# Feed-forward in groups of four, three and one token tiles in place of four, two and two

## The reference

```python
h = jnp.square(jax.nn.relu(jnp.einsum('bsd,fd->bsf', x, W_fc)))
y = jnp.einsum('bsf,df->bsd', h, W_proj)
# five steps of a neuron, from mem = 0:
#   mem = 0.9 * mem + y - (mem > 1);  spike = (mem > 1)
# result of the feed-forward: the sum of the five spikes / 5
```

## Time and profile before

| | |
|---|---|
| median of 3 runs | 1944.62 us (1941.21 to 1946.56) |
| profiled execution | 1942.4 us |
| its span | 1940.6 us |
| mean granted clock of PE | 0.984 |
| PE matmul busy | 1865.1 us, 96% |
| DVE busy | 1160.5 us, 60% |
| ACT busy | 834.9 us, 43% |
| POOL busy | 858.2 us, 44% |

### The profile page before, as it was taken

The page is one execution under the profiler, slowest core; times in us unless marked ns, Lnnn a source line. Parts: engine busy times, 40 slices in busy tenths (PEclk is TensorE's granted clock), DMA queues, the critical chain, the costliest instruction groups (busy, mean ns, idle before and its releaser), DMA issues. The chain is left out here.

```text
span 1940.6 us, 65596 instructions
## 1 busy us (share of the span) xinstructions
PE 1865.1 (96%) x28992; PEld 1605.5 (83%) x28992; DVE 1160.5 (60%) x1418; ACT 834.9 (43%) x1032; POOL 858.2 (44%) x830
## 2 busy tenths in 40 slices
PE   6999999999999999999999999999999989689998
PEld 3889898989888888888888989898989768567887
DVE  4375766657574848484848474757575561754265
ACT  4444444445453535353545354545444322324322
POOL 0192636454454536372727272727273520544111
PEclk9999999999999999999999999999999999879999
DMA  5200202011020202020202020202020130222110
GB/s 208 84 4 3 75 3 75 14 64 43 35 72 6 76 2 76 3 76 3 75 3 75 3 75 3 75 3 75 3 74 3 67 120 22 56 71 87 55 55 23
DMA packets 38829, 94.55 MB, mean 49 GB/s; under 512 B 18592, under 2 KB 18592, under 8 KB 38304
## 3 DMA queue, kind: packets, MB, share of 16 engines
q1 hardware_dynamic: 38560, 90.26, 13.5%
HBM read 81.99 MB, written 6.16 MB: 45 GB/s over the span
## 5 line engine op out<-in xcount | busy, mean ns | idle before, releaser
L378 POOL TENSOR_TENSOR fold<-fold,prob 128x256 f32<-128x256 f32 (+1 forms) x704 | 686.6, 975 | 55.2
L98 PE MATMUL ring<-y_parts,wk_s 128*128 128x402 f32 (+1 forms) x3072 | 609.1, 351 | 3.7 <-PEq L151 3.7
L98 PE MATMUL ring<-wv_s,y_parts 128*128 128x512 f32 (+1 forms) x2496 | 598.1, 397 | 0.0
L98 PEld LDWEIGHTS ring<-y_parts,wk_s 128*128 128x128 f32 x3072 | 553.0, 189 | 19.8 <-issue 6.0
L98 PEld LDWEIGHTS ring<-wv_s,y_parts 128*128 128x128 f32 (+1 forms) x2496 | 455.1, 184 | 113.2
L372 POOL TENSOR_TENSOR fold<-prob 128x256 f32<-128x256 f32 x64 | 66.4, 1037 | 729.9 <-ACT prob L415 729.9
L392 ACT ACTIVATE k_sb<-ring 128x402 f32<-128x402 f32 (+1 forms) x256 | 129.4, 506 | 376.5 <-PE ring L98 376.5
L528 DVE TENSOR_TENSOR prob<-prob,diag 128x1024 f32<-128x1024 f32 (+1 forms) x192 | 276.9, 1495 | 13.5 <-ACT diag L411 13.5
L405 ACT ACTIVATE prob<-s_ps 128x1536 f32<-128x1536 f32 (+1 forms) x128 | 199.9, 1562 | 137.9 <-PE s_ps L645 137.8
L415 ACT ACTIVATE prob<-prob 128x1024 f32<-128x1024 f32 (+1 forms) x192 | 206.7, 1123 | 0.9 <-DVE prob L528 0.9
L645 PEld LDWEIGHTS s_ps<-q_sb,k_sb 32*64 32x64 f32 x13312 | 155.9, 130 | 35.8 <-issue 35.8
(11 more groups left out here) (143 smaller groups left out, 1540.4 us busy)
## 6 DMA issues: line engine op xcount, KB each, us to landing
y_raw<-yT SPq DMA_DIRECT2D x48, 804.0 KB, 7.3
y_raw<-yT SPq DMA_DIRECT2D x16, 792.0 KB, 9.9
f_raw<-w_ffn SPq DMA_DIRECT2D x22, 512.0 KB, 3.2
p_x<-x SPq DMA_DIRECT2D x2, 1024.0 KB, 7.0
q_scratch<-p_x SPq DMA_DIRECT2D x4, 512.0 KB, 2.6
q_sb<-q_scratch SPq DMA_DIRECT2D x16, 128.0 KB, 7.8
x_sb<-x SPq DMA_DIRECT2D x4, 512.0 KB, 8.2
v_sw<-y_raw SPq DMA_DIRECT2D x4, 512.0 KB, 9.6
```

What stands on the lines that cost most here:

```text
L98: mm = pe.matmul(out, left(a, c), right(b, c), start=(c == 0 and n == 0), stop=(c == DC - 1 and n == 2))
L378: pool.tensor_tensor(acc[0:m], acc[0:m], prob[0:m, i, t, :], ALU.add).then_inc(sum_step, 1)
```

## The change

`GROUPS` becomes four, three and one tile, with banks 0 to 2 for the second group and bank 3 for the last. The moving side of the first layer is then 384 columns in the second group and 128 in the third. The last group's one tile has its neuron steps done in two halves of 256 columns that alternate, in place of two tiles of 512 that alternate, and they all wait for the last matmul; the semaphore `last_first` is gone.

```diff
--- before.py
+++ after.py
@@ -1153,9 +1153,9 @@
     FB = FF // P
     STEPS, BETA = 5, 0.9
 
-    GROUPS = [range(0, 4), range(4, 6), range(6, 8)]
+    GROUPS = [range(0, 4), range(4, 7), range(7, 8)]
     LAST_TILES = GROUPS[-1]
-    BANKS = [(0, 1, 2, 3), (0, 1), (2, 3)]
+    BANKS = [(0, 1, 2, 3), (0, 1, 2), (3,)]
     ALL = len(GROUPS) * FB
     LEVELS = spike_levels(STEPS, BETA)
     OPS = STEPS + 1
@@ -1189,7 +1189,6 @@
                                                           sem("f_sq"), sem("f_h_hi"), sem("f_h_lo"))
         y_part, y_out, spike, done, stored = (sem("f_y_part"), sem("f_y_out"), sem("f_spike"), sem("f_done"),
                                               sem("f_stored"))
-        last_first = sem("f_last_first")
         block = ctx.enter_context(nc.Block())
 
         def load_of(n):
@@ -1279,12 +1278,12 @@
 
         @block.vector
         def _(dve):
-            def neuron(t, k, y, total):
+            def neuron(t, k, y, total, at=slice(0, D)):
 
                 if k == 0:
                     return dve.tensor_scalar(total, y, LEVELS[0], None, ALU.is_gt)
                 if k == STEPS:
-                    return dve.scalar_tensor_tensor(x_sb[:, t, :], total, 1.0 / STEPS, x_sb[:, t, :],
+                    return dve.scalar_tensor_tensor(x_sb[:, t, at], total, 1.0 / STEPS, x_sb[:, t, at],
                                                     ALU.mult, ALU.add)
                 return dve.scalar_tensor_tensor(total, y, LEVELS[k], total, ALU.is_gt, ALU.add)
 
@@ -1347,18 +1346,16 @@
 
 
             q = OPS * LAST_TILES[0]
+            t = LAST_TILES[0]
+            dve.wait_ge(y_part, ALL)
             for k in range(OPS):
-                for j, t in enumerate(LAST_TILES):
-                    if k == 0 and j == 0:
-                        dve.wait_ge(last_first, 1)
-                    elif k == 0:
-                        dve.wait_ge(y_part, ALL)
+                for half in range(2):
+                    at = slice(half * D // 2, (half + 1) * D // 2)
                     dve.wait_ge(spike, q - 1)
-                    neuron(t, k, y_ps[BANKS[-1][j]][:], acc[:, 1 + j, :]).then_inc(spike, 1)
+                    neuron(t, k, y_ps[BANKS[-1][0]][:, at], acc[:, 1, at], at).then_inc(spike, 1)
                     q += 1
-            for j in range(len(LAST_TILES)):
-                dve.wait_ge(spike, q - 1 + j)
-                dve.sem_inc(done, 1)
+            dve.wait_ge(spike, q)
+            dve.sem_inc(done, 1)
 
         @block.tensor
         def _(pe):
@@ -1387,8 +1384,6 @@
                         mm = pe.matmul(y_ps[bank][:], h_s[:, n % HS, a, k * P:(k + 1) * P],
                                        place_of(load_of(n))[:, b, D:2 * D],
                                        start=(f == 0 and m == 0), stop=(f == FB - 1 and m == 2))
-                    if n == ALL - 1 and k == 0:
-                        mm.then_inc(last_first, 1)
                 mm.then_inc(y_part, 1)
 
             norm.pe_products(pe, range(TT - 2))
```

## The result

The changed kernel takes 1950.66 us (median of 22 runs, 1944.91 to 1960.83), the kernel before 1943.01 us (22 runs beside it, 1938.54 to 1949.56). The ratio is 1.0045 with a 95% interval from 1.0031 to 1.0060: slower by about 8.7 us (the medians lie 7.7 us apart), against the +5.4 us of the sum. The profiled execution of the changed kernel took 1946.96 us, its span is 1945.1 us: 4.5 us more than the span before.

What follows compares the result with a forecast made beforehand. PE, busy 96% of the span, was taken as the bound. Terms 9.8 - 2.9 + 1.0 + 0.2 - 2.5 - 0.2 = +5.4 us gave 1947.8, or 1950.0 us at the median; range 1943.0 to 1971.5.

Steps and rivals of the forecast that it cites:

- First layer, group of three: First-layer matmuls of 384 columns in the second group: half way between 1.42 and 2.72, 2.07 us a block, 33.1 us.
- First layer, last group: First-layer matmuls of 128 columns: 1.38 us a block, 22.1 us; both groups' first layers together +9.8 us.
- the load is the pace: Last group's first layer: weight load sets the matmul's pace, about 0.115 us each, so halving columns buys almost nothing.
- Rival B: Last group's first layer: narrow matmuls fall to the full-precision price, 2.7 us for 12; +25.4 us, 1970.0, chance 0.30.
- rival C: Last group's first layer: narrow matmuls as quick as their columns, 0.77 us for 12; -0.5 us, 1944.1, chance 0.15.
- Second layer: Second-layer matmuls of groups two and three: 192 of the same shape before and after, 0.23 us each, cost zero.
- The old stall gone: Second group: PE's 2.9 us of waits for f_h, with DVE held beside POOL's subtractions, disappear; -2.9 us, bounds -2.9 and 0.
- Rival D: Feed-forward: the stall between POOL and DVE stays or moves, 2.9 us kept; +8.3 us, 1952.9, slower, chance 0.10.
- The new waits: Last group: DVE late beside POOL in three blocks, +1.0 us, bounds 0 and 3; low half at the very end, +0.2.
- There each low half can wait for POOL: Last group, three blocks where POOL subtracts: DVE's low half of h is delayed, 0.3 to 0.4 us lost in each.
- The end: After the last matmul: twelve 256-column neuron steps take 4.2 us, -2.5 us; one store lands instead of two, -0.2.
- case A: The forecast itself: +5.4 us, 1950.0 at the median, own range 1947.5 to 1952.5, chance 0.42.

## Why the prediction was right, and where it was off

- **First layer, group of three:** 2.07 us a block forecast, 2.10 measured.
- **First layer, last group:** 1.38 forecast from the load's pace, 1.29 measured. The step "the load is the pace" is shown by the two runs that double the columns and the loads. Its price was taken between 0.109 and 0.118; it is 0.1075. Rival B, the full-precision price (2.7 us), and rival C (0.77 us) are out. The line through 256 and 512 columns ends where the load begins.
- **Second layer:** forecast zero, measured +0.7 us: 0.74 for three matmuls, not 0.69. The term was mis-sized. Three matmuls take 0.69 to 0.70 when matmuls of 256 columns go before, 0.74 after 128 and 0.78 after 64, so it lies in the change from narrow matmuls to wide ones.
- **The old stall gone:** -2.9 forecast, -3.4 measured. The mechanism held, and the size was the idle time between records, which is less than what a wait costs from start to start. Rival D is out for the group of three.
- **The new waits:** +1.0 for the low half beside POOL and +0.2 at the end were forecast; 2.1 and 0.3 came. The step that fell short is "There each low half can wait for POOL": the last neuron step of a tile can too, since it adds to x and reads two operands from SBUF. It fell beside POOL and cost 1.2 us, as the run that holds it back shows. Nor is 0.3 to 0.4 us a limit for the low half: with three steps a block it waited for most of a subtraction, and PE 1.78 us.
- **The end:** -2.5 and -0.2 forecast, -2.6 and -0.2 measured.
- **The sum:** +5.4 forecast, +5.9 in the profiles. That they lie so near is in part luck: the first layers came 1.0 us under their term and the stall 0.5 under, the second layer 0.7 and the new waits 1.2 over. The 1950.0 us forecast at the median, beside 1950.66 measured, is luck as well: it stands on a median of the kernel before that was 1.6 us above that of the 22 runs. The rest of the measured +8.7 us (1.0045, 1.0031 to 1.0060) was in no term: I costed one execution, at full clock, and gave no chance to a fall of the clock in the last group. It is shown that such a fall is possible there (half clock from a gap of 1.78 us on, about +12 us). That the upper group of the changed kernel is this same fall was not seen in a trace and stays open: in all six profiles with the gap of 1.2 us the clock stays full, and that no run of 12 without this gap lies in the upper group can be chance.
- **The chances:** case A was given 0.27 for no difference and 0.15 for slower. The mechanism was A's, and the time came out on the slower side, just beyond the 0.3% that I had named.

## What to carry to other kernels

In this number format, with the weights standing for one matmul only, a matmul of 64 or 128 columns costs as much as its weight load (by the line through 256 and 512 columns, an estimate, anything below some 230 does); splitting tokens unevenly into groups makes the narrow group pay that in full, and here a shorter end (2.6 us) was bought with 16 x 12 matmuls that shrink by a tenth for half the columns (+8.8 us for both groups together). Before regrouping work to shorten a tail, look at what stalls in the middle: moving neuron steps away from POOL's subtractions gave 0.2 to 0.3% with no change of PE's work. And on an engine that shares a port, sort the instructions by where their operands lie, one by one, the last of a series too.

## What the runs showed of the hardware that was not expected

- A matmul of 64 columns and one of 128 follow each other at the same 0.108 us when each has its own load.
- PE keeps its full clock in an unbroken stream of blocks of 24 matmuls of 64 columns and 3 of 512, but in the run with three steps a block it fell to 1.2 GHz after a wait of 1.78 us in the last group and stayed there to the end of PE's work; of the 26 us from 1925 to 1951 PE was busy 25.8. After a wait of 1.90 us between blocks with 256 columns, in the kernel before, it stayed full.
- What a wait of PE costs is more than the idle time between its records: 3.4 us for 2.9.
- Waiting for one's own previous step on DVE costs 0.02 us between instructions of 0.70 us, so a step every 0.72 us; two tiles' steps that alternate follow at 0.60 (4.78 us for 8 in the earlier trace rows).
